# 64 more pairs as batch-row units, their row sums on three engines, and the last layers in half steps (pairwise interaction tower, one core)

## The reference, cut to what matters

```python
# B = 2048, F = 40 fields, D = 64; 780 pairs (i < j); all float32
e = stack([tbl_f[ids[:, f]] for f in range(40)], axis=1)       # (2048, 40, 64)
viW = einsum('bpd,pde->bpe', e[:, i_idx, :], W)                # W: (780, 64, 64)
z = einsum('bpe,bpe->bp', viW, e[:, j_idx, :])                 # (2048, 780)
h = concatenate([z, dense_ctx], axis=1)                        # (2048, 796)
h = maximum(h @ W_top1 + b_top1, 0)                            # 512
h = maximum(h @ W_top2 + b_top2, 0)                            # 256
y = h @ W_top3                                                 # (2048, 1)
```

## Time and profile before

| what | value |
|---|---|
| median of 3 runs | 1160.86 us (1159.98 to 1162.97) |
| span of the profiled execution | 1158.4 us |
| TensorE busy | 1128.4 us, 97% of the span |
| VectorE busy | 980.5 us, 85% |
| ScalarE busy | 915.8 us, 79% |
| GpSimd busy | 694.9 us, 60% |
| chain that ended last | TensorE 78%, ScalarE 9%, VectorE 7%, issue 5%, DMA 1% |
| granted TensorE clock | full |

### The profile page before, as it was taken

The page is one execution under the profiler, slowest core; times in us unless marked ns, Lnnn a source line. Parts: engine busy times, 40 slices in busy tenths (PEclk is TensorE's granted clock), DMA queues, the critical chain, the costliest instruction groups (busy, mean ns, idle before and its releaser), DMA issues.

```text
span 1158.4 us, 46094 instructions
## 1 busy us (share of the span) xinstructions
PE 1128.4 (97%) x17504; PEld 411.4 (36%) x17504; DVE 980.5 (85%) x899; ACT 915.8 (79%) x6965; POOL 694.9 (60%) x834
## 2 busy tenths in 40 slices
PE   6999998999999999999999999999999999999999
PEld 2323333333333333333333333333333333333333
DVE  8699999999866789999975779999986678999970
ACT  1598899889575879999766688999956688999961
POOL 7765565555667667777667656766666666641200
PEclk9999999999999999999999999999999999999999
DMA  6323232232313123232322223323231322322200
GB/s 175 107 71 91 63 90 72 56 89 69 82 46 86 49 67 90 69 89 72 92 51 72 55 59 82 76 65 91 69 87 42 83 48 66 90 57 73 58 14 0
DMA packets 70667, 82.92 MB, mean 72 GB/s; under 512 B 15728, under 2 KB 59520, under 8 KB 70316
## 3 DMA queue, kind: packets, MB, share of 16 engines
q1 hardware_dynamic: 50960, 60.01, 17.8%
q0 software_dynamic: 19456, 19.96, 9.1%
q10 hardware_dynamic: 32, 0.01, 0.0%
HBM read 79.91 MB, written 0.01 MB: 69 GB/s over the span
## 4 chain that ended last, share of the span: by engine, by line
PE 78%; ACT 9%; DVE 7%; issue 5%; DMA 1%; SPq 0%; DVEq 0%
PE Ups L872 31%; PE Zps L892 16%; PE Ups L865 15%; PE Ups L914 9%; ACT PB L653 7%; DVE P L788 4%; PE Ups L851 3%; PE Ups L836 3%; PE Ups L921 2%; DVE PB L777 2%; ACT P L674 1%; DMA V<-tbl 1%; DVE zB L746 1%; ACT V L661 0%; PE Ups L902 0%
## 5 line engine op out<-in xcount | busy, mean ns | idle before, releaser
L653 ACT ACTIVATE PB<-PB 128x64 f32<-128x64 f32 x3408 | 815.3, 242 | 71.8 <-DVE PB L777 68.6
L788 DVE TENSOR_TENSOR P<-Ups,V 128x1024 f32<-128x1024 f32 x504 | 599.0, 1216 | 94.8 <-PE Ups L872 92.4
L633 POOL DMA_INDIRECT stage<-tbl,idx x512 | 485.5, 948 | 278.7 <-PE Ups L872 96.5
L653 ACT ACTIVATION_READ_ACCUMULATOR PB<-PB 128x1 f32 x3408 | 641.4, 188 | 0.0
L872 PE MATMUL Ups<-V,wf 64*32 64x512 f32 x8384 | 535.4, 591 | 10.6 <-ACT V L661 4.6
L777 DVE TENSOR_TENSOR PB<-Ups,VN 128x1024 f32<-128x1024 f32 x256 | 311.8, 1218 | 23.6 <-PE Ups L865 21.2
L892 PE MATMUL Zps<-P,sel 64*32 64x512 f32 x4192 | 282.4, 590 | 0.0
L865 PE MATMUL Ups<-wf,V 64*32 64x512 f32 x4096 | 275.6, 590 | 3.6 <-ACT V L661 2.2
L872 PEld LDWEIGHTS Ups<-V,wf 64*32 64x32 f32 x8384 | 152.3, 106 | 290.3 <-issue 165.5
L608 POOL TENSOR_TENSOR PB<-PB 128x512 f32<-128x512 f32 (+4 forms) x160 | 97.6, 610 | 69.4 <-DVE PB L777 58.6
L892 PEld LDWEIGHTS Zps<-P,sel 64*32 64x32 f32 x4192 | 80.9, 107 | 138.6 <-issue 134.4
(11 more groups left out here) (37 smaller groups left out, 196.5 us busy)
## 6 DMA issues: line engine op xcount, KB each, us to landing
wf<-w_units SPq DMA_DIRECT2D x336, 160.0 KB
stage<-tbl,idx POOLq DMA_INDIRECT x512
V<-tbl SPq DMA_DIRECT2D x8, 250.0 KB
w1s<-w SPq DMA_DIRECT2D x1, 1792.0 KB, 8.9
VN<-tbl,idx POOLq DMA_INDIRECT x96, 2.6
w2s<-w SPq DMA_DIRECT2D x1, 512.0 KB, 8.6
idx<-ids SPq DMA_DIRECT2D x1, 240.0 KB, 15.1
z<-dense_t SPq DMA_DIRECT2D x4, 32.0 KB, 3.0
```

The source lines that it names most:

```text
L633: pool.indirect_dma_start(out=natural_rows(m, t)[:, D * f:D * f + D], out_offset=None, in_=tables[field][:, :], in_offset=bass.IndirectOff ...
L653: last = act.activation(p, p, ACT.Copy, accum_out=zB[:, t, at:at + 1])
L788: dve.tensor_tensor(p, Ups[:, slot, :, :rows], v, ALU.mult).then_inc(mul_done, 1)
```

## The change

Sixteen a units of every group (slots 12 to 15 against the last four pairs gathered, 3 to 0: 64 field pairs) become sixteen row units `("c", k, t)`, k in 15, 14, 13, 12. The gathered rows of pairs 3 to 0 are kept in natural order in a new tile `VL` (one buffer for the four pairs). 195 units per group remain, now 115 a or d and 80 b or c; the quads go from 66 to 58 and the parts from three to two, so that the z0 join goes away. Row units stand closer: one for every 1.32 a units.

Their sums are shared out anew: after group 0 by `SUM_TURN`, 14 of 20 on ScalarE, 3 on GpSimd, 3 on VectorE (before: 5 of 6 on ScalarE, 1 of 6 on GpSimd). In group 0, row units 0 to 39 keep 5 of 6 on ScalarE and 1 on VectorE, and from the fortieth on a pattern of ten has 7, 1 and 2 (GpSimd 2, VectorE 1; written "AAPAADAAPA"). Over group 0 this makes 61 sums on ScalarE (before 53), 11 on VectorE (before 11), 8 on GpSimd (before none).

There are two ztr steps per group, the second for the c columns and the dense inputs, which are now loaded to `zB`. The last layers run in half steps of 256 columns: 13 steps per group, eight of seven matmuls 10 units apart, four of four and the last 14 units apart. The GpSimd scratch for transfers is set to 8192.

```diff
@@ row_items, ready, ramp_units, group_units
-    out += [("a", k, jp) for jp in range(last - 1, k, -1)]
+    out += [("a", k, jp) for jp in range(last - 1, k, -1) if not (k < LATE and jp in C_KEYS)]
...
-RAMP_TO, A_LAST = 10, 8
+RAMP_TO, A_LAST, POOL_FROM, AHEAD = 10, 2, 40, 3
...
+def ready(item, k):
+    return k <= (AHEAD if item[0] == "c" else item[1] + AHEAD)
...
-        if i < len(b_items) and a >= a0 + apart * (i - i0) and b_items[i][1] >= a_items[a][1]:
-            out.append((b_items[i], i % 6 != 5))
+        if i < len(b_items) and a >= a0 + apart * (i - i0) and ready(b_items[i], a_items[a][1]):
+            out.append((b_items[i], "AAAAAD"[i % 6] if i < POOL_FROM else "AAPAADAAPA"[i % 10]))
...
+    b_items += [("c", k, t) for k in C_KEYS for t in range(TILES[g])]
...
-        while i < len(b_items) and a >= 3 + 1.86 * i:
+        while i < len(b_items) and a >= 3 + 1.32 * i:
@@ parts, sums, steps
-PART_ENDS = (QUADS - 2 * PART, QUADS - PART, QUADS)
+PART_ENDS = (QUADS - PART, QUADS)
...
+SUM_TURN = "AAAPAADAAAPAADAAPAAD"
+def sums_by(i):
+    return RAMP_SUMS[i] if i < len(RAMP_SUMS) else SUM_TURN[(i - len(RAMP_SUMS)) % len(SUM_TURN)]
...
-MLP_STEPS = N1 // P128 + N2 // P128 + 1
+HALF = GB // 2
+L1_STEPS, L2_STEPS = 2 * N1 // P128, 2 * N2 // P128
+MLP_STEPS = L1_STEPS + L2_STEPS + 1
...
-MLP_APART = 10
+MLP_APART, LAST_APART = 10, 14
...
+def ztr_at(g, x):
+    return min(B_AT[b_end(g, x) - 1] + 7.2, TOTAL - 0.7)
...
-    return at + 0.01 * (m + 1) if g == GROUPS - 1 else int(at) + 8.6 + MLP_APART * m
+    if g == GROUPS - 1:
+        return at + 0.01 * (m + 1)
+    return int(at) + 8.6 + MLP_APART * min(m, L1_STEPS) + LAST_APART * max(m - L1_STEPS, 0)
@@ GpSimd, VectorE
+                if r == PAIRS - LATE and g:
+                    pool.wait_ge(mul_done, U0[g])
...
-                    v = VN[:, g % 2, unit[2]:unit[2] + 1, :].to_broadcast([P128, 2, WB_COLS])
+                    v = VN[:, g % 2, unit[2]:unit[2] + 1, :] if unit[0] == "b" else VL[:, unit[2]:unit[2] + 1, :]
+                    v = v.to_broadcast([P128, 2, WB_COLS])
...
-                if n in Z0_BEFORE:
-                    g = Z0_BEFORE[n]
-                    z0 = z[:, z0_tile(g), :SIZES[g]]
-                    dve.wait_ge(z0_copied, g + 1)
-                    dve.tensor_tensor(z0, Zps[:, 1, :SIZES[g]], z0, ALU.add).then_inc(z0_done, 1)
@@ TensorE: second ztr, half steps
+                    for h in range(1 if x else 2):
+                        at, rows = (B_PAIRS, C_ROWS) if x else (P128 * h, P128)
                         for t in range(TILES[g]):
-                            last = pe.transpose(Ups[:, slot, h, P128 * t:P128 * (t + 1)],
-                                                zB[:, t, P128 * h:P128 * (h + 1)], ident[:, :])
+                            last = pe.transpose(Ups[:rows, slot, h, P128 * t:P128 * (t + 1)],
+                                                zB[:, t, at:at + rows], ident[:, :])
...
-                        last = pe.matmul(Ups[:, slot, 0, :size], w1s[:, k % ZT, P128 * x:P128 * (x + 1)], z[:, k, :size],
-                                         start=n == 0, stop=n == ZT - 1)
+                        last = pe.matmul(Ups[:, slot, 0, :HALF], w1s[:rows, k, P128 * m:P128 * (m + 1)],
+                                         z[:rows, k, cols], start=n == 0, stop=n == ZT - 1)
...
-                        last = pe.matmul(Ups[:, slot, 0, :size], w2s[:, k, P128 * (x - 4):P128 * (x - 3)],
-                                         h1[:, k, :size], start=k == 0, stop=k == 3)
+                        last = pe.matmul(Ups[:, slot, 0, :HALF], w2s[:, k, P128 * m:P128 * (m + 1)],
+                                         h1[:, k, cols], start=k == 0, stop=k == 3)
@@ kernel
-    nc = bacc.Bacc("TRN2", target_bir_lowering=False, num_devices=1)
+    nc = bacc.Bacc("TRN2", target_bir_lowering=False, num_devices=1, dynamic_dma_scratch_size=8192)
```

More of the change, by code:

```diff
@@ L121, in z_place, with z_column, z_columns_free @@
     part, at = z_part(block // 4)
-    if part == 0:
-        return 32 * (block % 4) + at + PART_ENDS[0] * half, 0
-    return 32 * (block % 4) + at, 2 * part - 1 + half
+    return 32 * (block % 4) + at, 2 * part + half
+def z_column(unit):
+    if unit[0] == "b":
+        return 4 * JP * (B_ROWS - 1 - unit[1])
+    return B_PAIRS + 4 * LATE * C_KEYS.index(unit[1])
+def z_columns_free(g, unit):
+    return 2 * g - (unit[0] == "b")
 def quad_units(q):
@@ L336, in schedule @@
     steps += [(red_at(q), ("red", *divmod(q, QUADS))) for q in range(GROUPS * QUADS)]
-    steps += [(ztr_at(g), ("ztr", g, 0)) for g in range(GROUPS)]
+    steps += [(ztr_at(g, x), ("ztr", g, x)) for g in range(GROUPS) for x in range(2)]
     steps += [(mlp_at(g, m), ("mlp", g, m)) for g in range(GROUPS) for m in range(MLP_STEPS)]
@@ L377, in schedule @@
         for extra in range(max(room, 1)):
-            if issued == GROUPS * PAIRS or step[0] == "ztr" or not stage_free(issued, pair):
+            if issued == GROUPS * PAIRS or step[0] == "ztr" or not room_for(issued, pair, count["main"]):
                 break
@@ L420, with z_rows, build @@
 Z_COUNT = {s: n + 1 for n, s in enumerate(Z_STEPS)}
[L421 to L427 removed]
 def z_tiles(step):
[L431 to L434 removed]
+    if step[0] == "z":
+        return (2 * step[2], 2 * step[2] + 1)
+    return (ZB_TILE + 2,) if step[2] else (ZB_TILE, ZB_TILE + 1)
+def z_rows(tile):
+    return C_ROWS if tile == ZT - 1 else P128
+def build(nc, ids, ids_hot, tables, dense, w_units, w1, b1, w2, b2, w3, y):
     fp32, i32 = mybir.dt.float32, mybir.dt.int32
@@ L489, in build @@
         natural = [sem(f"natural{n}") for n in range(JP)]
+        late = [sem(f"late{n}") for n in range(LATE)]
         wf_loaded = [sem(f"wf_loaded{n}") for n in range(W_SLOTS)]
@@ L890, in _ @@
                             rows = slice(D * h, D * h + D)
-                            to = at if part else at + PART_ENDS[0] * h
-                            last = pe.matmul(Zps[out, h, :size], sel[rows, 31 - to:63 - to],
+                            last = pe.matmul(Zps[out, h, :size], sel[rows, 31 - at:63 - at],
                                              P[rows, a % P_SLOTS, strip % 2, :size],
@@ L896, in _ @@
                 elif kind == "ztr":
-                    pe.wait_ge(sums_act, act_sums(B0[g + 1]))
-                    pe.wait_ge(sums_dve, dve_sums(B0[g + 1]))
-                    wait(pe, sums_pool, pool_sums(B0[g + 1]))
-                    for h in range(2):
+                    end = b_end(g, x)
+                    pe.wait_ge(sums_act, act_sums(end))
+                    pe.wait_ge(sums_dve, dve_sums(end))
+                    wait(pe, sums_pool, pool_sums(end))
+                    if x:
+                        pe.wait_ge(dense_loaded, 16 * (g + 1))
@@ L964 @@
             w1[row, tile] = W1[pair(i, j)[0]]
-    for k in range(B_ROWS):
+    for unit in [("b", k) for k in range(B_ROWS)] + [("c", k) for k in C_KEYS]:
         for b in range(2):
             for j in range(2 * JP):
-                at = 4 * JP * (B_ROWS - 1 - k) + 2 * JP * b + j
-                w1[at % P128, ZB_TILE + at // P128] = W1[pair(2 * k + b, 2 * J0 + j)[0]]
+                at = z_column(unit) + 2 * JP * b + j
+                n = pair(2 * unit[1] + b, j + 2 * J0 if unit[0] == "b" else j)[0]
+                w1[at % P128, ZB_TILE + at // P128] = W1[n]
     pairs = F * (F - 1) // 2
-    w1[DENSE_ROW:DENSE_ROW + DENSE, 0] = W1[pairs:]
+    w1[C_PAIRS:C_ROWS, ZT - 1] = W1[pairs:]
     arrays = {
@@ L988 @@
     y = nc.dram_tensor("y", [B, 1], mybir.dt.float32, kind="ExternalOutput").ap()
-    build(nc, t["ids"], t["ids_hot"], [t[f"tbl_{f}"] for f in range(F)], t["dense_t"], t["w_units"], t["w1"], t["b1"],
+    build(nc, t["ids"], t["ids_hot"], [t[f"tbl_{f}"] for f in range(F)], t["dense"], t["w_units"], t["w1"], t["b1"],
           t["w2"], t["b2"], t["w3"], y)
```

199 lines of the change are left out of this document (104 added, 95 removed).

## The result

The changed kernel takes 1256.52 us (median of four runs, 1255.89 to 1257.27), the kernel before, on the same chip beside it, 1161.91 us. The ratio is 1.0818 (95% interval 1.0805 to 1.0831): 95 us slower. The forecast was 1170, 1148 to 1186. The sign was right, the size wrong by a factor of ten, and the time lies far outside the range.

What follows compares the result with a forecast made beforehand. TensorE was taken to bound groups 1 to 3, with TensorE, VectorE and ScalarE all near full in group 0. Group 0 +9, groups 1 to 3 0, end +0.5 us gave span 1167.9, median 1170 us, range 1148 to 1186.

Steps and rivals of the forecast that it cites:

- nothing, and a few us in group 1 if the marks hold them back: Gathers for the new row units' earlier need of pair 0: no cost, at most a few us in group 1.
- the fifth: Rival: gathers stall waiting for their landing, total over 1200 us; chance 0.01.
- VectorE, +4.0 us a group: Groups 1 to 3: row sums added to VectorE make it the bound in dense units, +4.0 us per group.
- the count of 48 units at VectorE's rate: Units 0 to 10 and 147 to 188 of a group run at VectorE's pace, 0.083 us more each.
- Coupling, +0.8: Groups 1 to 3: nearly full engines block each other through three PB and three PSUM slots, +0.8 us per group.
- TensorE, -4.3 a group: Groups 1 to 3: eight red steps fewer -6.9, second ztr step +0.75, six more switches +1.9 us.
- The switch: Last layers: each further change between step kinds on TensorE costs 0.31 us, six more per group, +1.9 us.
- Group 0, +9 (2 to 18): ScalarE's row sums lengthen group 0: +8 us in units 34 to 101, +1 in units 101 to 195.
- rival 4: Last layers: 256-column records do not cover weight loads, 27 us a group, total 1280 us; chance 0.04, 0.01 in full.
- Scratch: Smaller GpSimd transfer scratch costs nothing unless gathers wait for landing, 2.6 us each in place of 0.95.
- Rivals 1 and 2: TensorE's saving comes back, VectorE's loss not showing, 1150 us (chance 0.2); or nothing to measure, 1161 us (chance 0.18).
- Rival 3: Engines block each other everywhere: +4.6 us a group, group 0 +15, total 1190 us; chance 0.07.

Runs made afterwards that it cites:

- e4_space: Changed kernel with the planner's spacing of gathers at 1.5 us in all groups (changed kernel: 1.5, 1.6, 1.7, 1.8): 1200.72 us, ratio 1.034.
- e3_full: Changed kernel with the last layers back in whole steps of 512 columns, 7 per group: 1199.35 us, ratio 1.033.
- b2_half: Kernel before with only the last layers in half steps, 13 per group: 1343.97 us, ratio 1.024, where the kernel before took 1309.73 us.
- f1_both: Changed kernel with gathers spaced 1.5 us and five row sums of group 0 moved from ScalarE to VectorE: 1188.07 us, ratio 1.023.
- f3_no_dve_sums: f1_both with VectorE's row sums in groups 1 to 3 left out, their columns set to zero: 1160.56 us, ratio 0.999.
- f4_pool: f1_both with VectorE's row sums of groups 1 to 3 given to GpSimd: 1210.48 us, ratio 1.043.
- g3_one_dve: f2_both_full with 1 of 20 sums on VectorE, 4 on GpSimd, 15 on ScalarE (before it 3, 3, 14): 1201.22 us, ratio 1.035.
- f2_both_full: f1_both with the last layers in whole steps: 1183.77 us, ratio 1.019.
- g1_before_shares: Kernel before with only the changed shares of row sums after group 0, moving 28 sums to VectorE: 1179.9 us, ratio 1.016.

## Why the prediction was wrong, by its own steps

The 95.7 us of span, from the runs (each from the totals of one set): late gathers 54.6, group 0's ScalarE sums 12, the sums on VectorE 27.5, together 94; the 1.6 that remain hold TensorE's saving, the switches, the second transpose step and whatever the scratch costs.

- **Gathers: "nothing, and a few us in group 1 if the marks hold them back".** This step failed, and made more than half of the error: 54.6 us where nothing stood (the rival nearest to it, the fifth, had a chance of 0.01). I compared rates, one pair per 16 us against 8 us of issue time, and looked at group 1, where the first group's head start still helps. The rate was never the limit; the order was. The planner lets gathers pass only where it thinks there is room, and the halved steps have room for one where there was room for three; the closer row units delay them too. A delay of 16 units in group 1 became one of 24 in group 2 and a starved TensorE in group 3. e4_space shows that even spacing alone cures it, e3_full that whole steps alone do, b2_half that half steps alone bring it about. The constants 1.9 and 3.08 stood in `schedule()` and `step_us()` and were not worked through.
- **VectorE, +4.0 us a group.** The mechanism (what TensorE saves is handed to VectorE) held, and its sign too: in units 147 to 188 of group 1 of f1_both VectorE is busy 98%, and TensorE 97% where it had 100%. The size was off by more than two: 9.2 us a group measured (f1_both to f3_no_dve_sums). The step that mis-sized it took units 10 to 147, beside the last layers, as TensorE's, by averages over 10 or 14 units; 6.6 of the 8.6 us found in group 1 lie there. The chain shows a stretch of 11 us of VectorE's inside them. So the term that failed is the count of 48 units at VectorE's rate.
- **Coupling, +0.8.** It can't be told apart from the term above by these runs. GpSimd's and ScalarE's worse results as takers of the sums (f4_pool, g3_one_dve) say that neither has room for them.
- **TensorE, -4.3 a group.** 512 records fewer at L944 are there. Without VectorE's sums the groups are 277.0, 275.5 and 264.6 against 276.6, 274.4 and 268.2: of 12.9 us, 2.1 are seen, all in group 3. The steps themselves did get shorter. Added up from the start of each step to the start of the next without idle time, groups 1 and 2 of f3_no_dve_sums spend 8.0 us less than before on red steps, z transposes and last layers together, where 8.6 were forecast. Against that stand 2.4 us more on units, 3.2 on pair transposes (four more pairs fall into these two groups) and 3.6 more of idle time (6.2 against 2.6). Its units 147 to 188 of group 1 take 50.8 us, before 49.8, with ScalarE busy 98% and VectorE 97%: the chain there is ScalarE's sums for 20% and VectorE for another 20%, where before it was TensorE alone, so even without VectorE's sums the other two set part of the pace. The switch was priced high rather than low: in f1_both a half step takes 3.22 us from its start to the next step's in most cases, 0.17 over 14 records of 0.218, and the step behind 0.88 in place of 0.86, 0.19 in all where 0.31 stood. By whole against half steps (f1_both against f2_both_full) the six further switches of a group are worth 4.3 us over three groups, 1.4 each group, where 1.9 stood; that is inside the forecast's own error.
- **Group 0, +9 (2 to 18).** The total came out inside its range, +13.7, and in part by luck, since its two terms were off in opposite ways. Units 34 to 101 took 101.9 us where they had taken 86.5: +15.4, outside the +3 to +12 that stood for them. Units 101 to 194 took 120.4 against 122.1: -1.6 where +1 stood. The cause is the one named, ScalarE: it is full (19.98 of 20 us from 120 to 140), though at 93% over these units and not at the 97% that was to show it, and moving five sums away gives 12.3 us back. What I missed as well is that TensorE's waits came with a lower clock (0.98 over 90 to 178 us).
- **Half records (rival 4).** Rightly left out: 0.218 us against the 0.216 forecast, over 112 records. By the rule of the Trainium skill (TensorE: Matmul & The Clock Gate, The mechanism) that only a load into another row group overlaps a matmul, the loads would have stood in the open, by rival 4's estimate 27 us a group; this trace does not agree, since a full-array load of 0.190 us leaves no trace in a pitch of 0.218. The Trainium skill (the same title, Step-by-step: what each phase is for) also says that TensorE pulls a load ahead of running matmuls when it goes to the background weight buffer; that is the statement which the 0.218 us agree with.
- **Scratch.** As forecast, no stall: a gather's issue is 0.95 us before and after. Its effect on the total was measured only on the odd chip, +1.1% [0.4, 1.9] by two runs, and is not settled; f3_no_dve_sums has the small scratch too and takes what the kernel before takes.
- **Rivals 1 and 2** said that sums slip into VectorE's idle time; f3_no_dve_sums and g1_before_shares show that 61 to 68% of their length does not. Rival 3 (1190) is near what the kernel takes once the gathers are in time and group 0 is relieved, 1188, but by other terms (it had +15 in group 0 and +4.6 in each later group, where f1_both has +2.9 and +9.2, +10.7, +5.2): a coincidence.

## What to carry to other kernels

Where an order is written ahead of time by a planner, a change of a step's size changes what the planner lets happen beside it; print its slack per transfer before and after, down to the last group, since lateness adds up over groups. Two engines whose work per item is nearly the same (here 1.19 and 1.22 us a unit by the forecast's own sum) can take turns as the bound within microseconds: work added to the second cost 0.6 to 0.7 of its duration here, at 81 to 86% busy by the averages. A saving on the engine that shows 97% counts only as far as the next ones have room in the same few units.
